# The relative-position band product of an attention stage, taken one query tile per pair instead of two in every second half of a step

## What is computed

```python
# x: 8 x 1024 x 256, 16 heads of 16; rel_pe: 129 x 16; K = 64
qkv = q @ in_proj_weight.T + in_proj_bias
qh = qh / math.sqrt(d)
scores = jnp.einsum('bhid,bhjd->bhij', qh, kh)
rel = jnp.clip(pos[None, :] - pos[:, None], -K, K) + K
bias_r = jnp.einsum('bhid,rd->bhir', qh, rel_pe)
bias = jnp.take_along_axis(bias_r, rel, axis=-1)
attn = jax.nn.softmax(scores + bias, axis=-1)
out = jnp.einsum('bhij,bhjd->bhid', attn, vh)
```

## Time and profile before

| What | us |
|---|---|
| median of three runs | 2544.59 |
| the profiled execution | 2541.43 |
| its span on the core | 2539.5 |
| busy: TensorE matmul | 2255.9 |
| busy: VectorE | 1748.5 |
| busy: ScalarE | 1660.6 |
| busy: GpSimd | 626.0 |

### The profile page before, as it was taken

One profiled execution on the slowest core, in us unless ns is written; L12 is line 12 of the kernel. 1 busy time (PEld: TensorE's weight loads), 2 busy tenths in 40 slices (PEclk: granted clock), 3 DMA queues, 4 the chain that ended last, 5 costly groups with the idle time before them and its releaser, 6 DMA issues. The chain is left out here.

```text
span 2539.5 us, 46740 instructions
## 1 busy us (share of the span) xinstructions
PE 2255.9 (89%) x14642; PEld 1243.8 (49%) x14642; DVE 1748.5 (69%) x3444; ACT 1660.6 (65%) x1982; POOL 626.0 (25%) x1117
## 2 busy tenths in 40 slices
PE   4996589999999999999999999999999998599997
PEld 3554234444444444444444444444444443488886
DVE  3443457777777777777777777777777773488885
ACT  2432157777777777777777777777777776266766
POOL 0001111222122221221212221222212210466673
PEclk9998589999999999999999999999999999799999
DMA  6997767777777777777777776777777760433321
GB/s 194 364 342 269 184 183 190 201 200 195 195 196 195 192 201 193 194 202 192 194 193 199 200 194 192 196 204 193 195 195 197 198 183 14 120 96 103 108 80 42
DMA packets 452026, 468.55 MB, mean 185 GB/s; under 512 B 106901, under 2 KB 410726, under 8 KB 451942
## 3 DMA queue, kind: packets, MB, share of 16 engines
q1 hardware_dynamic: 355830, 368.91, 49.6%
q0 software_dynamic: 83072, 89.92, 15.4%
q10 hardware_dynamic: 13040, 8.80, 1.2%
HBM read 244.73 MB, written 221.25 MB: 183 GB/s over the span
## 5 line engine op out<-in xcount | busy, mean ns | idle before, releaser
L819 ACT ACTIVATE probs<-weigh_ps 128x1024 f32<-128x1024 f32 x1024 | 1047.2, 1023 | 375.2 <-PE weigh_ps L985 373.9
L945 PE MATMUL ring_ps<-keys,queries 48*128 48x512 f32 x2048 | 832.0, 462 | 27.9 <-DVE partial_max L860 18.1
L871 DVE CUSTOM_DVE_ANT_1 ring_ps<-ring_ps,band_all 128x512 f32<-128x512 f32 x1008 | 681.0, 715 | 229.0 <-PE ring_ps L945 228.7
L860 DVE TENSOR_REDUCE partial_max<-ring_ps 128x2 f32<-128x1024 f32 x512 | 627.7, 1226 | 282.9 <-PE ring_ps L945 238.8
L985 PE MATMUL weigh_ps<-queries,keys 50*128 50x512 f32 (+3 forms) x2688 | 735.0, 379 | 0.9 <-ACT probs L819 0.6
L1002 PE MATMUL sum_ps<-probs,values 128*32 128x512 f32 x4096 | 546.7, 605 | 0.2 <-ACT probs L819 0.2
L945 PEld LDWEIGHTS ring_ps<-keys,queries 48*128 48x128 f32 x2048 | 363.5, 187 | 351.7 <-issue 171.4
L970 PE MATMUL weigh_ps<-ident,band_all 128*128 128x128 f32 x2048 | 362.0, 289 | 125.9 <-ACT band_out L807 113.1
L807 ACT ACTIVATE band_out<-weigh_ps 128x1024 f32<-128x1024 f32 x256 | 261.8, 1024 | 188.8 <-PE weigh_ps L933 162.8
L970 PEld LDWEIGHTS weigh_ps<-ident,band_all 128*128 128x128 f32 x2048 | 216.6, 141 | 325.0 <-ACT band_out L807 189.1
L985 PEld LDWEIGHTS weigh_ps<-queries,keys 50*128 50x128 f32 x2688 | 357.6, 186 | 17.0 <-ACT probs L819 8.9
(11 more groups left out here) (110 smaller groups left out, 1746.0 us busy)
## 6 DMA issues: line engine op xcount, KB each, us to landing
band_scr<-band_out SPq DMA_DIRECT2D x256, 512.0 KB, 5.1
band_all<-band_scr SPq DMA_DIRECT2D x128, 512.0 KB, 4.5
band_all<-band_scr SPq DMA_DIRECT2D x128, 256.0 KB, 3.2
keys<-k_scr POOLq DMA_DIRECT2D x128, 240.0 KB, 8.5
k_scr<-k_parts SPq DMA_DIRECT2D x16, 1792.0 KB, 8.0
q_scr<-q_parts SPq DMA_DIRECT2D x16, 1024.0 KB, 6.3
queries<-q_scr POOLq DMA_DIRECT2D x128, 128.0 KB, 3.2
o_scr<-weighted_s SPq DMA_DIRECT2D x64, 256.0 KB, 5.6
```

Of the source, the lines that this page charges most:

```text
L819: nc.scalar.activation(probs[:, u % PROBS], weigh_ps[weigh_of["scores", at]][:], ACT.Exp).then_inc(s_pr, 1)
L860: nc.vector.reduce_max(partial_max[:, g, :, e, 0], ring_ps[:, first:second + 1], AX_X).then_inc(s_seen, HG)
L871: nc.vector.tensor_tensor_reduce(out=both, in0=both, in1=bias, scale=1.0, scalar=LOWEST, op0=ALU.add, op1=ALU.max, accum_out=partial_max[: ...
L945: nc.tensor.matmul(dst, query_rows(c, h, ROWS, tile * P, (tile + 1) * P), key_rows(c, h, ROWS, c0, c0 + 512), start=True, stop=True, tile_ ...
```

## The change

The band product works on one query tile instead of two, so it fills half of a weighing buffer (2 x 256 columns) with 2 matmuls. It is done in all eight pairs of a step. It stands directly behind the first unit's products, ahead of the weighted sum. The numbering stays continuous over steps: pairs 4 to 7 make tiles 0 to 3 of the heads three steps ahead, and pairs 0 to 3 of the next step make tiles 4 to 7. ScalarE copies each half by itself into its half of the `band_out` place. A chunk is still two tiles for the DMAs, and is written in every odd pair at `u` = 3, 7, 11 or 15, behind the read of the chunk before. In the table of buffers every pair now has three fillings, so in all pairs the two units share a buffer, also where no band is left to make.

```diff
             def bands_at(step, m):
-                return m >= QT and 0 <= step + BAND_STEPS < G
+                return 0 <= band_index(step, m) < G * NT
             def band_index(step, m):
-                return (step + BAND_STEPS) * NM + m - QT
+                return (step + BAND_STEPS) * NT + m - QT
...
-                        if what[0] == "scores" or m >= QT:
-                            weighs += 1
+                        weighs += 1
...
                 def write_bands(i, n):
-                    sp.wait_ge(s_be, cnt(i, NM, n + 1))
+                    sp.wait_ge(s_be, cnt(i, NT, 2 * n + 2))
...
-                    if u == 0 and bands_at(step - 1, NT - 1):
-                        read_bands(i, band_index(step - 1, NT - 1))
-                    if u % 2 and bands_at(step, m):
-                        if bands_at(step, m - 1):
-                            read_bands(i, band_index(step, m - 1))
-                        write_bands(i, band_index(step, m))
+                    if u % 4 == 3:
+                        chunk = band_index(step, m) // 2
+                        if 0 <= chunk - 1 < G * NM:
+                            read_bands(i, chunk - 1)
+                        if 0 <= chunk < G * NM:
+                            write_bands(i, chunk)
...
                 def copy_band(i, n):
-                    act.wait_ge(s_bp, cnt(i, NM, n + 1))
-                    if n >= BANDS_OUT:
-                        act.wait_ge(s_bw[n % BANDS_OUT], cnt(i, 16 * NM // BANDS_OUT, 16 * (n // BANDS_OUT)))
-                    nc.scalar.activation(band_out[:, n % BANDS_OUT].rearrange("p h e c -> p h (e c)"),
-                                         weigh_ps[weigh_of["band", n]][:], ACT.Copy).then_inc(s_be, 1)
+                    chunk, e = n // 2, n % 2
+                    act.wait_ge(s_bp, cnt(i, NT, n + 1))
+                    if e == 0 and chunk >= BANDS_OUT:
+                        act.wait_ge(s_bw[chunk % BANDS_OUT], cnt(i, 16 * NM // BANDS_OUT, 16 * (chunk // BANDS_OUT)))
+                    nc.scalar.activation(band_out[:, chunk % BANDS_OUT, :, e], weigh_ps[weigh_of["band", n]][:, :, 0:2 * P],
+                                         ACT.Copy).then_inc(s_be, 1)
...
                 def band_product(i, n):
-                    c, m = n // NM, n % NM
-                    if m == 0:
+                    c, tile = n // NT, n % NT
+                    if tile == 0:
...
-                    for e in range(2):
-                        tile = 2 * m + e
-                        for h in range(HG):
...
+                    for h in range(HG):
...
                     products(i, step, m, 0)
-                    lagging(i, step, m)
                     if bands_at(step, m):
                         band_product(i, band_index(step, m))
+                    lagging(i, step, m)
```

More of the change, by code:

```diff
@@ L911, in wait_for @@
                         else:
-                            pe.wait_ge(s_be, cnt(i, NM, n + 1))
+                            pe.wait_ge(s_be, cnt(i, NT, n + 1))
                 def seen_count(n):
@@ L927, in band_product @@
                     dst = weigh_ps[weigh_of["band", n]]
-                    for e in range(2):
-                        tile = 2 * m + e
-                        for h in range(HG):
[L931 to L935, removed]
+                    for h in range(HG):
+                        table = rel_terms[h * ROW_TILE:h * ROW_TILE + ROWS, :].rearrange("p (a c) -> p a c", a=3)
+                        moving = table[:, 0:3:2] if tile == NT - 1 else table[:, 0:2]
+                        last = nc.tensor.matmul(dst[:, h, 0:2 * P].rearrange("p (a c) -> p a c", a=2),
+                                                query_rows(c, h, ROWS, tile * P, (tile + 1) * P), moving,
+                                                start=True, stop=True, tile_position=(h * ROW_TILE, 0))
                     last.then_inc(s_bp, 1)
```

## The result

The changed kernel takes 2607.38 us (median of four runs, 2593.20 to 2630.03) against 2545.39. The ratio is 1.0257, with a 95% interval of 1.0220 to 1.0294. It is slower by 62 us, where 2441 was forecast and 2503 was the upper end of the range. The profiled execution was the slowest of the four, at 2630.03 us.

The account below looks back on a forecast made before the run. No engine was full; TensorE, nearest, was bound by its order and waits. Per step 26.26 + 1.6 + 0.6 - 0.7 - 0.8 = 27.0 us against 28.71, -105 us over 61 steps, +2 at the end: 2441 us, range 2387 to 2503.

Parts of the forecast that it names:

- SyncE's queue, "I count 0": SyncE's blocking band reads and writes: four loops take 26.5 us, fit the new step with 0.5 to spare, cost 0.
- Its point of decision: SyncE's four loops: a slowdown was to begin once they exceed 28.7 us, the second disturbed loop passing 7.8 us.
- the sum would be void if the clock fell: Sign to check: the granted clock should stay at 1.00, otherwise the summed forecast does not hold.
- The wait for the copy of the band in four pairs: TensorE's transposes wait for ScalarE's band copy in pairs 4 to 7: 2.2 us a step, expected to go.
- The new one in pair 1: TensorE waits in pair 1 because ScalarE's `copy_sums` delays the band's copy: +0.6 us a step (0.1 to 0.6).
- Tile products: Eight one-tile band products a step on TensorE, 0.20 us each: +1.6 us a step (1.0 to 2.7).
- The copies: ScalarE's eight half-size band copies a step, 0.60 us each, hidden in seven pairs.
- the waits that I took off, 0.7 and 0.8: Per step on TensorE: 0.7 us of shared-buffer waits covered by the product, 0.8 us of bank waits in three pairs gone.
- the ring's floor: Chain of reduction, look, transposes, looks, reduction: about 3.17 us against TensorE's pair of 3.18, so no more gain was taken.
- the switch of tiling: Changing tiling mode drains TensorE; the new place adds no switch, so a tile costs 0.12 us, 0.6 us a step lower.
- Slower: Rival, 6%: band writes straddle GpSimd's query and key loads, a second loop takes 8 us, chain 29.0 us; 2564 us.
- The DMA chain or the ring takes the gain: Rival, 22%: SyncE's chain needs 28 us and rows come late, or the bank wait stays with 0.22 us tiles; 2503 us.

Follow-up runs that it names:

- reads_late: The changed kernel with each band chunk read back 3 half pairs later, so SyncE no longer blocks on a landing ahead of the maxima's rows; 2467.44 us, 0.9702.
- tile_product_twice: The changed kernel with each chunk read back 3 half pairs later, plus each tile product issued twice into the same place; 2595.37 us, 1.0216.

## Why the prediction was wrong

**The step that failed: SyncE's queue, "I count 0".** I had read that the chain had hardly any spare time, summed its four loops to 26.5 us with one of them disturbed by GpSimd's loads, and gave the case of two disturbed ones 6% and a price of +18 us. The second loop was disturbed: 8.87 and 10.14 us where I had 5.4 and 10.04, a sum of 29.6. The writes at `u` = 15 and `u` = 3 (issued at 1235.97 and 1244.33) do straddle the loads of queries and of keys, as that rival said; that the loads are what stretches them is read from the times, as no run moved the loads. Its point of decision was wrong as well. I took 28.7 us, the old step. But a chain that is longer than TensorE's own step, 27.6 us, falls behind in every step. By my own numbers the decision was at the 27.0 that I forecast, and 26.5 had half a microsecond of slack.

The record of before already spoke against the 26.5. Its spare time of 46.4 us in 1600 us is 0.8 us a step, so the chain filled 27.9 of the 28.7 us: more than a step of 27.0 or 27.6 has. Rows 9 alone, with 4.2 us in 320, say as much. That was with the writes in their old places, but it was the one chain on record. I read the row as "nearly full", and then put four loops together to a shorter chain that no row showed.

**Its price was mis-sized.** A chain of 29.6 us would give 29.6 us a step if TensorE only waited. It took 30.2. The lag is paid in stops of 1.3 to 6.8 us, one per two to four steps, and behind all but one of them the clock stood at 0.50 for a while: 8 us in the stretch shown, in which half of the matmuls were done. Over the steps 1 to 59 the loss is (30.13 - 27.6) x 59 = 149 us. TensorE's waits for the rows in these steps are 80 us (the 89.4 of the page count the steps around them as well). The rest of 70 us I put down to the lower clock and to the restart; no run tells these two apart. The Trainium skill (TensorE: Matmul & The Clock Gate, HAM oscillation) describes this pattern for matmuls between waits for DMAs: the clock falls in the wait and the slow matmuls behind it are paid each time. The trace agrees on the cost, with 31 matmuls against 61 in 8 us, and only in part on the moment: the clock is 0.82 within the stop shown, but in nine others it falls behind the stop. I had written that the sum would be void if the clock fell, and gave that no chance of its own.

**What the forecast said of TensorE held, by and large.** Undisturbed steps are 27.6 us against 27.0. The wait for the copy of the band in four pairs went. The new one in pair 1 came, at 0.6 us as priced: pair 1 takes 3.82 us and 3.23 without it. Tile products cost 0.19 on average where I took 0.20. The copies take 0.59 where I took 0.60. The miss is in the waits that I took off, 0.7 and 0.8: pair 2 stayed at 3.18 and pairs 6 and 7 at the 3.36 and 2.96 they have in step 61, as expected, but pairs 0 and 3 grew from 3.29 to 3.75 and from 3.16 to 3.41. Behind pair 3, at the first looks of pair 4, TensorE waits for a bank of the ring, 19.4 us in 58 steps, 0.33 each. That is the ring's floor that I had named. In pair 0 there is no such wait; the tile costs 0.34 there, and the rest of its 0.46 stays open.

**On the switch of tiling.** The rule that I cited from the Trainium skill (TensorEngine Tiling (Array Packing), Key Properties) would have made a tile worth 0.12. The rows say 0.11 to 0.13 in four pairs and 0.24 to 0.34 in the other four, 0.19 on average; the measurement decides. What sets the pairs apart no run shows.

**The rivals.** "Slower" was the right mechanism at 6%; its time was 43 us too low. "The DMA chain or the ring takes the gain" had the same cause. The error was to price the chain as if it could only cap the gain.

**For what it is worth, the change works with one swap on SyncE**: 2469.93 us, and 2431.91 with late reads and the copies in the other order, against my 2441. The move without the split is as good at 2427.90 (the intervals of the two ratios overlap).

## What to carry to other kernels

Before a change that shortens the bounding engine's step, sum the serial chain of every queue that blocks on landings, per step, and compare it with the new step and not the old one. The old step less the queue's waits for its producers gives the chain at once: here 28.7 - 0.8 = 27.9 us. A queue that hardly ever waits for its producers is already full. Put the next write ahead of the read that blocks on the last one, or read one place later; it moves no byte and here it is worth 137 us. When a steady loop gets slower on average, look at single steps first: 27.6 and 36.4 us tell more than 30.2.

## What the runs showed of the hardware beyond expectation

A stop of TensorE of 5.93 us was followed by 8 us at a granted clock of 0.50, so that stops cost more than their length. Short ones did it too: behind a stop of 1.52 us (at 1957.65) the clock is 0.79 on average over 8 us, and during it it was 1.00. In `reads_late` no wait of TensorE in the steady stretch is over 0.7 us, and the clock stays at 1.00.

Sixteen more matmuls per step, 64 more in the loop of four steps, brought a wait of up to 3.9 us in `tile_product_twice` about once per turn of the loop, with five times the packets on the instruction queue (157 against 30). The packets carry 2.57 MB against 0.49, which is 0.14 MB more for each of the 15 turns. No other kernel here has it.

The same write of 512 KB took 3.6 us to land in one place of a step of the changed kernel (issued at 1260.99) and 9.7 us in another (1244.33), with GpSimd's loads of keys and values, a read of the band and the store of the sums under way.
